# Two attention layers' projections: from whole-array stages to streams of four tiles, with folded spin weights

## Reference

```python
h = emb[x]                                       # token ids -> 2048 rows of 256
q, k, v = h @ Wq.T + bq, h @ Wk.T + bk, h @ Wv.T + bv      # 16 heads of 16
h = (softmax(q k^T / 4) v) @ Wo.T + bo           # attention 1 ("tok")
y = layernorm(h)
q, k, v = y @ Wq.T + bq, y @ Wk.T + bk, y @ Wv.T + bv      # attention 2 ("attn")
s  = q @ Wqs.T + bqs                             # 3 numbers per head
c  = cross(k @ Wks.T + bks, v @ Wvs.T + bvs)
h  = h + softmax((q k^T + s c^T) * temp) v @ Wo.T + bo
```

## Time and profile before

| | us |
|---|---|
| median of 3 runs | 4443.97 (4440.75 to 4445.12) |
| profiled execution | 4443.18, its span 4441.2 |
| busy in the span: PE, DVE, ACT, POOL | 4048.9, 3197.5, 2627.5, 1930.9 |
| first score of attention 1 | 128.03 |
| end of attention 1 | about 536.0 |
| first score of attention 2 | 735.01 |
| end of attention 2 | about 1143.5 |
| rest (output projection 2, feed-forward, recurrence, six layers) | 3298 |

### The profile page before, as it was taken

One profiled execution on the slowest core, in us unless ns is written; L12 is line 12 of the kernel. 1 busy time (PEld: TensorE's weight loads), 2 busy tenths in 40 slices (PEclk: granted clock), 3 DMA queues, 4 the chain that ended last, 5 costly groups with the idle time before them and its releaser, 6 DMA issues. The chain is left out here.

```text
span 4441.2 us, 98171 instructions
## 1 busy us (share of the span) xinstructions
PE 4048.9 (91%) x33142; PEld 2813.6 (63%) x33144; DVE 3197.5 (72%) x5533; ACT 2627.5 (59%) x7011; POOL 1930.9 (43%) x1276
## 2 busy tenths in 40 slices
PE   4899967999445699999999999999999999999997
PEld 2566633666313377777777777777777777777776
DVE  3788644888677677777777777777777777777775
ACT  1476522677231476666666666666666666666664
POOL 2000010000000566666566666665666666666663
PEclk9899987999777899999999999999999999999999
DMA  4222023221010310021011110111001100111001
GB/s 114 73 54 57 21 66 81 55 53 48 20 40 29 104 23 18 20 59 40 18 23 46 46 27 18 39 41 40 20 21 49 51 18 20 51 42 29 20 18 48
DMA packets 101814, 184.23 MB, mean 41 GB/s; under 512 B 25173, under 2 KB 59121, under 8 KB 100977
## 3 DMA queue, kind: packets, MB, share of 16 engines
q1 hardware_dynamic: 100592, 176.37, 14.9%
q0 software_dynamic: 768, 2.10, 0.3%
HBM read 99.51 MB, written 25.17 MB: 28 GB/s over the span
## 5 line engine op out<-in xcount | busy, mean ns | idle before, releaser
L1542 POOL TENSOR_TENSOR swp<-raw,table 128x512 f32<-128x512 f32 x384 | 481.1, 1275 | 635.0 <-DVE ss L1953 634.9
L705 DVE TENSOR_REDUCE maxima<-PS 128x1 f32<-128x512 f32 x1024 | 631.6, 680 | 129.9 <-PE PS L539 129.5
L1625 PE MATMUL PS<-wqk,xT 128*128 128x512 f32 x1536 | 686.5, 600 | 5.7 <-DMA wqk<-in_L_ffn_Wqkv 4.4
L1572 POOL TENSOR_TENSOR probs<-probs,prob_recip 128x512 f32<-128x512 f32 x384 | 472.7, 1250 | 437.5 <-DVE prob_recip L2011 437.5
L1882 ACT ACTIVATE probs<-probs,neg 128x128 f32<-128x128 f32 x1536 | 595.9, 389 | 27.1 <-DVE neg L2005 25.6
L669 ACT ACTIVATE probs<-PS 128x512 f32<-128x512 f32 x1024 | 519.2, 602 | 153.8 <-PE PS L553 153.3
L1552 POOL TENSOR_TENSOR rinv<-ssm,power 128x32 f32<-128x32 f32 x96 | 526.9, 5489 | 0.0
L1625 PEld LDWEIGHTS PS<-wqk,xT 128*128 128x128 f32 x1536 | 283.7, 190 | 336.0 <-issue 253.0
L1728 PE MATMUL PS<-xnT,w 128*128 128x128 f32 x3840 | 476.9, 275 | 0.4 <-DVE hidden L2071 0.4
L539 PE MATMUL PS<-k_stack,q_stack 128*128 128x512 f32 x1024 | 428.1, 438 | 36.4 <-DMA k_stack<-L_attn_qk 17.8
L1728 PEld LDWEIGHTS PS<-xnT,w 128*128 128x128 f32 x3840 | 452.3, 192 | 1.4 <-issue 0.7
(11 more groups left out here) (231 smaller groups left out, 8089.2 us busy)
## 6 DMA issues: line engine op xcount, KB each, us to landing
V_window<-V SPq DMA_DIRECT2D x180, 256.0 KB, 2.8
wqk<-in_L_ffn_Wqkv SPq DMA_DIRECT2D x12, 1024.0 KB, 6.4
w<-in_L_ffn_W SPq DMA_DIRECT2D x18, 640.0 KB, 4.7
q_stack<-L_tok_qk SPq DMA_DIRECT2D x128, 80.0 KB
k_stack<-L_tok_qk SPq DMA_DIRECT2D x128, 80.0 KB
q_stack<-L_attn_qk SPq DMA_DIRECT2D x128, 80.0 KB
k_stack<-L_attn_qk SPq DMA_DIRECT2D x128, 80.0 KB
wv<-in_L_ffn_Wqkv SPq DMA_DIRECT2D x6, 1024.0 KB, 5.1
```

What stands on the lines that cost most here:

```text
L705: dve.tensor_reduce(maxima[:, k // 2, k % 2:k % 2 + 1], SM(r, k), AX.X, ALU.max).then_inc(sm_maxed, 1)
L1542: pool.tensor_tensor(swp[:, w, :, a:a + LD // 2], raw[:, w, :, b:b + LD // 2], table[:, j % 2, 2 + w, a:a + LD // 2].rearrange("p (o d) -> ...
L1572: pool.tensor_tensor(view, view, psr[:, 4 * q:4 * q + 4].rearrange("p (h o) -> p h o", o=1) .to_broadcast([P, 4, P]), ALU.mult).then_inc(p ...
L1625: mm = pe.matmul(wide(kind, half, j), xT[:, k, at:at + P], rhs, start=(k == 0), stop=(k == DC - 1))
```

## The change

`softmax_attention`, `project`, `embed` and `load_constants` go; `attentions` calls `token_projections`, `attend`, `spin_projections`, `attend`, `output_projection`.

- `token_projections` is one block. The ids are loaded first, then constants and all weights of both attentions. Each pair of tiles has its own gather semaphore; PE interleaves transposes (`turn`), query/key units and values by pair. ACT fills the two ring tensors with zeros (two operations), DVE fills V's pads, and after chunk 0 the upper 32 partitions of `ks` with ones. Values are added with their bias two tiles at a time. Behind the 16 units' stores SP issues the loads of heads 0 to 5 in the same block.
- `spin_projections` is one block with attention 1's output projection (pairs of tiles, one PSUM bank), layernorm by chunk (GpSimd's power on 4 columns), and attention 2's projections by chunk. The five spin weights are multiplied into the projection weights once (`fold`), so that the five spin products take XT as input; the feature-major values (L351, L385) go. ACT does the copies of transposes. The spin stores are in two groups of six. It too ends with the loads of heads 0 to 5.
- `attend` leaves the loads of heads 0 to 5 out. Stacks have 16 or 19 rows, no rows of zeros or ones are stored; the row of the maxima is partition 127, and the products for the maxima use partitions 0 to 111 or 0 to 114. `output_projection` serves attention 2 alone, with the bias added ahead of the wait.

```diff
-ROWS = 20
...
+def stack_loads(c, eng, at, scratch, it, r, rows, loaded):
+    qs, ks = at
+    for blk in range(4):
+        for dst, part in ((qs, blk // 2), (ks, 2 + blk % 2)):
+            eng.dma_start(dst[32 * blk:32 * blk + rows, r, :].bitcast(F32),
+                          scratch[part, bass.ds(it, 1), 0:rows, :].rearrange("o r s -> (o r) s")).then_inc(loaded[r], 16)
...
+def token_projections(c, V, qs, ks, scratch, loaded, w, spin_w):
...
+                    load_output_weights(c, sp, "L0_tok", w, wo_loaded)
+                    load_spin_weights(c, sp, spin_w)
+                for n, (ch, which, m) in enumerate(units):
+                    b, off = ch // 2, (ch % 2) * CH
+                    it0 = b * HEADS + m * HPC
+                    for half, (src, ready) in enumerate(((high, qk_high), (low, qk_low))):
+                        sp.wait_ge(ready, n + 1)
+                        sp.dma_start(scratch[2 * which + half, it0:it0 + HPC, 0:HD, off:off + CH],
+                                     src[:, n % 2, :].bitcast(F32)).then_inc(stored[n % 2], 16)
+                for u in range(2):
+                    sp.wait_ge(stored[u], 32 * len(units) // 4)
+                sp.wait_ge(cleared, 3)
+                for r in range(RING):
+                    stack_loads(c, sp, (qs, ks), scratch, r, r, HD, loaded)
+                for u in range(2):
+                    sp.wait_ge(stored[u], 32 * len(units) // 2)
+                sp.wait_ge(wo_loaded, 32)
...
+                turn(0)
+                turn(1)
+                for ch in range(CHUNKS):
+                    for u in range(4):
+                        query_key(4 * ch + u)
+                        if u in (0, 2) and ch + 1 < CHUNKS:
+                            turn(2 * ch + 2 + u // 2)
+                        if u in (1, 3):
...
+                nothing = c.ident[:, :].rearrange("p (o f) -> p o f", o=1).to_broadcast([P, RING * SEQ // P, P])
+                act.activation(qs[:, :, :].rearrange("p r (a f) -> p (r a) f", f=P), nothing, ACT.Copy, scale=0.0).then_inc(cleared, 1)
+                act.activation(ks[:, :, :].rearrange("p r (a f) -> p (r a) f", f=P), nothing, ACT.Copy, scale=0.0).then_inc(cleared, 1)
...
+                    act.wait_ge(qk_done, n + 1)
+                    wait(act, qk_low, n - 1)
+                    wait(act, stored[n % 2], 32 * (n // 2))
+                    act.activation(whole[:, n % 2, :], c.PS[:, 4 + n % 2, :], ACT.Identity, bias=bias, scale=by).then_inc(qk_whole, 1)
+                    act.activation(high[:, n % 2, :], c.PS[:, 4 + n % 2, :], ACT.Identity, bias=bias, scale=by).then_inc(qk_high, 1)
...
+                dve.memset(V[:, :, :, HD:HD + 1], 1.0)
+                dve.memset(V[:, :, :, HD + 1:VW], 0.0)
...
+                for ch in range(CHUNKS):
+                    for u in range(4):
+                        if u in (1, 3) and ch + 1 < CHUNKS:
+                            take(2 * ch + 2 + u // 2)
+                        split(4 * ch + u)
+                        if u in (1, 3):
+                            add_bias(2 * ch + u // 2)
+                    if ch == 0:
+                        dve.wait_ge(cleared, 2)
+                        dve.memset(ks[96:P, :, :].bitcast(F32), 1.0).then_inc(cleared, 1)
...
+def spin_projections(c, V, qs, ks, scratch, loaded, context, w, s):
...
+                    if n % 4 == 3:
+                        for which2 in range(2):
+                            sp.wait_ge(spin_split, 2 * ch + which2 + 1)
+                            for half, src in enumerate((s_high, s_low)):
+                                for comp in range(3):
+                                    sp.dma_start(scratch[2 * which2 + half, b * HEADS:(b + 1) * HEADS, HD + comp, off:off + CH],
+                                                 src[32 * comp:32 * comp + HEADS, which2, :].bitcast(F32)).then_inc(spin_stored, 16)
+                for u in range(2):
+                    sp.wait_ge(stored[u], 32 * len(units) // 4)
+                sp.wait_ge(spin_stored, 16 * 12 * CHUNKS // 2)
+                for r in range(RING):
+                    stack_loads(c, sp, (qs, ks), scratch, r, r, HD + 3, loaded)
...
+                def out_projection(g):
+                    pe.wait_ge(c_taken, g + 1)
+                    wait(pe, added, g)
...
+                def fold(i):
+                    wait(pe, fold_out, 2 * (i - 1))
+                    for d in range(DC):
+                        for k in range(DC):
+                            pe.matmul(c.PS[:, 6 + i % 2, d * 96:(d + 1) * 96], s["raw"][:, origin[i], k, d * P:(d + 1) * P], s["stacks"][:, i, k, :],
+                                      start=(k == 0), stop=(k == DC - 1))
...
+                def spin(ch, i):
+                    n = spins * ch + i
+                    if n < 2:
+                        pe.wait_ge(fold_out, 2 * spins)
+                    wait(pe, spin_out, n - 1)
+                    for k in range(DC):
+                        mm = pe.matmul(c.PS[0:96, 6 + n % 2, :], folded[:, i, k, :], XT[:, ch % 2, k, :], start=(k == 0), stop=(k == DC - 1))
...
+                def project_chunk(ch):
+                    query_key(4 * ch)
+                    spin(ch, 0)
+                    query_key(4 * ch + 1)
+                    spin(ch, 1)
+                    values(2 * ch)
+                    query_key(4 * ch + 2)
+                    spin(ch, 2)
+                    query_key(4 * ch + 3)
+                    spin(ch, 3)
+                    values(2 * ch + 1)
+                    spin(ch, 4)
+                def out_chunk(ch):
+                    turn("c", 2 * ch)
+                    turn("c", 2 * ch + 1)
+                    out_projection(2 * ch)
+                    out_projection(2 * ch + 1)
+                out_chunk(0)
+                out_chunk(1)
+                pe.wait_ge(s["loaded"], 16 * SPIN_LOADS)
+                for i in range(spins):
+                    fold(i)
+                turn("x", 0)
+                turn("x", 1)
+                out_chunk(2)
+                project_chunk(0)
+                turn("x", 2)
+                turn("x", 3)
+                out_chunk(3)
+                project_chunk(1)
+                turn("x", 4)
+                turn("x", 5)
+                project_chunk(2)
+                turn("x", 6)
+                turn("x", 7)
+                project_chunk(3)
...
+                def split_spins(ch, which, src):
+                    wait(dve, spin_stored, 16 * 12 * ch)
+                    dve.tensor_copy(s_high[:, which, :], src).then_inc(spin_high, 1)
+                    dve.wait_ge(spin_high, 2 * ch + which + 1)
+                    dve.tensor_tensor(s_low[:, which, :], src, s_high[:, which, :].bitcast(F32), ALU.subtract).then_inc(spin_split, 1)
...
+                def project_chunk(ch):
+                    split(4 * ch)
+                    dve.wait_ge(spin_out, spins * ch + 1)
+                    split_spins(ch, 0, five[:, 0, :])
+                    split(4 * ch + 1)
+                    add_bias(2 * ch)
+                    split(4 * ch + 2)
+                    split(4 * ch + 3)
+                    add_bias(2 * ch + 1)
+                    cross_products(ch)
+                    split_spins(ch, 1, cross[:, :])
...
+                out_chunk(0)
+                dve.wait_ge(s["loaded"], 16 * SPIN_LOADS)
+                dve.tensor_scalar(bqs[:, :], s["bqk"][:, 0, :], s["factor"][:, 0:1], None, ALU.mult).then_inc(scaled, 1)
+                norm(0)
+                out_chunk(1)
+                for i in range(spins):
+                    dve.wait_ge(fold_done, i + 1)
+                    dve.tensor_copy(folded[:, i, :, :], c.PS[:, 6 + i % 2, 0:DC * 96].rearrange("p (d n) -> p d n", d=DC)).then_inc(fold_out, 1)
+                    dve.tensor_tensor(fold_bias[:, i:i + 1], c.PS[0:96, 6 + i % 2, DC * 96:DC * 96 + 1], s["sbias"][:, i:i + 1], ALU.add).then_inc(fold_out, 1)
+                dve.wait_ge(fold_out, 2 * spins)
+                dve.tensor_scalar(fold_bias[:, 0:1], fold_bias[:, 0:1], s["factor"][0:96, 0:1], None, ALU.mult).then_inc(scaled, 1)
+                out_chunk(2)
+                norm(1)
+                project_chunk(0)
+                norm(2)
+                out_chunk(3)
+                project_chunk(1)
+                norm(3)
+                project_chunk(2)
+                project_chunk(3)
...
+    KMAX = 96 + rows
...
-                sp.dma_start(qs[0:1, r, :].rearrange("o (a t) -> o a t", a=QT).bitcast(F32),
+                sp.dma_start(qs[P - 1:P, r, :].rearrange("o (a t) -> o a t", a=QT).bitcast(F32),
...
-                if h0:
+                if h0 and not (isinstance(t, int) and t < RING):
...
-                pe.matmul(SM(r, k), qs[:, r, q * P:(q + 1) * P], ks[:, r, half * CH:(half + 1) * CH],
+                pe.matmul(SM(r, k), qs[0:KMAX, r, q * P:(q + 1) * P], ks[0:KMAX, r, half * CH:(half + 1) * CH],
...
+            attentions(c)
```

(28 more changed lines are left out.)

594 lines of the change are left out of this document (373 added, 221 removed).

## The result

The changed kernel takes 4773.22 us (median of four runs, 4771.72 to 4778.74) where the kernel before takes 4442.36 (four runs, 4438.96 to 4445.12): a ratio of 1.0747 [1.0729, 1.0766], 331 us slower. 4363 had been forecast, with a range of 4342 to 4392. The prediction was wrong, in sign and far outside its range.

The account below looks back on a forecast made before the run. PE bounds the attention loops, which stay; PE's idle time in the projection stretches was to shrink. 4443.2 - 27.5 (part A) - 53.6 (part B) = 4362.1 us, 4363 as median, range 4342 to 4392.

Parts of the forecast that it names:

- What costs nothing: Attention loops and second output projection: fewer stack rows and the loads cost nothing, loops stay at 408 us.
- Part B: End of attention 1 to first score of attention 2: 145.4 us instead of 199.0, a gain of 53.6.
- 48 loads, 17.9: Stack loads of six heads ending the block before attention 2: 17.9 us, at a pitch of 0.373 us.
- wrong if: Signs of failure: chunk period above 26, fold over 12 us, clock in B under 0.9, a score waiting for a load.
- part A: Start to first score of attention 1: 100.5 us instead of 128.0, a gain of 27.5.
- rival (b): Less gain: first gathers stand behind 3 MB of weights, B's chunks still paced by stores; 4389 us, chance 0.15.
- rival (a): More gain: store cycle shortens to PE's 2.9 us, loads issue at 0.33, allowances unused; about 4345 us, chance 0.15.
- The fills: Part A: ACT's two ring fills 5.5 us each, off the path; DVE's fill of `ks` 5.2, 3.4 on the path.
- Rival (c): Slower: short pauses keep PE at 1.2 GHz throughout the projections; 4502 us, chance 0.05.
- the row of the pitch: Stack loads: 0.373 us per 80 KB load is the issuing queue's time, so 48 issues hold the block 17.9 us.

Follow-up runs that it names:

- E1: The changed kernel with attention 2's loads at 20 rows instead of 19, the added row zeros stored once at the start: 4363.32 us.
- D1: E1 with 17 rows in attention 1 and 21 in attention 2 instead of 16 and 20: 4705.24 us.
- D2: E1 with 18 rows in attention 1 and 24 in attention 2 instead of 16 and 20: 4384.62 us.
- E4: The changed kernel with each 19-row load of attention 2 issued as two, of 16 and 3 rows: 4376.88 us.
- E5: E1 with only head 0 loaded ahead of each attention, heads 1 to 5 at the head of the loop: 4333.34 us.
- E6: E5 with head 0's eight loads put among the last stores of each projection block: 4324.03 us, 0.9733 of the kernel before.
- E3: The kernel before with loads of 19 rows instead of 20 in attention 1 alone: 4834.85 us.
- E2: The changed kernel with attention 2's scratch laid out in planes of 20 rows, loads still taking 19: 4772.78 us.

## Why the prediction was wrong, step by step

**The step that failed** is "What costs nothing": "Rows of the stacks fall from 20 to 16 or 19 ... the loads of the loop are hidden (DMA share 0.20, rows 1)". I asked what fewer rows cost PE and took it for granted that a load with less data can't take longer. The share of 0.20 was read as slack of a whole; how many of the 16 engines one load uses was never asked. The same fault is in Part B's "48 loads, 17.9": the 0.373 us of the earlier trace rows belongs to loads of 20 rows, and the new ones are not of that kind. With 19 rows, 129 us took the place of 17.9, and 710 that of 408. No rival held this; the "wrong if" did name the symptom (a score that waits for a load in spite of the prefetch). The trace of before had a hint, in the row of 729.5 us above: loads alone, issued faster than they land, and still a share of 0.64 (80 KB every 0.373 us are 220 GB/s issued, and 147 were moved). The price of the cause, 76 KB at one engine's pace, stands in no row of before.

**The rest of the sum held, in part by luck.** E1 has the 20 rows for which the sum was in effect made, and takes 4363.32 us; the sum gave 4363. By the marks of the table above, E1 gains 29.0 us in part A (27.5 forecast) and 55.8 in part B (53.6), and loses 2.7 in the two loops and 2.9 in the rest, where the sum had nothing; the differences nearly cancel. The parts, in the trace of after:

- Part A: first score at 100.70, forecast 100.5, but errors cancel. The first ACT copy came at 23.40 (21.6 forecast). From it to the sixteenth took 51.3 us, not 57.7, and the last store was out at 77.16 instead of 82.0. The 48 loads gave the 5 us back: with 16 rows their pitch is 0.48 us, not the 0.373 of 20 rows, 22.9 us instead of 17.9.

```profile
23.40 0.69 ACT L258 ACTIVATE whole<-PS,bqs 128x512 f32<-128x512 f32 x1 [8.56 <-issue]
...
34.91 0.69 ACT L258 ACTIVATE whole<-PS,bqk 128x512 f32<-128x512 f32 x1 [7.99 <-DMA tok_qk<-low]
...
42.12 5.18 DVE L311 MEMSET k_stack<- 32x6144 f32 x1 [1.34 <-issue]
...
50.24 0.69 ACT L258 ACTIVATE whole<-PS,bqk 128x512 f32<-128x512 f32 x1 [5.72 <-DMA tok_qk<-low]
...
74.74 0.69 ACT L258 ACTIVATE whole<-PS,bqk 128x512 f32<-128x512 f32 x1 [0.45 <-PE PS L219]
...
76.83 0.33 SPq L180 DMA_DIRECT2D tok_qk<-low  x1
77.28 0.38 SPq L132 DMA_DIRECT2D q_stack<-tok_qk  x1
```

- The 51.3 us are themselves a sum in which errors cancel. The step to the third unit takes 9.25 us instead of 3.48, since ACT waits for the first unit's store: 5.8 us lost, where 2 were allowed for sharing with the weights. The DMA share is 0.93 from 22 to 36 us, and with more stores of zeros ahead this wait grows (none in after, 8.0 us; 12 in D1, 12.5 us; 28 in D2, 24.6 us), so rival (b)'s queue was there, though at the first stores and not at the gathers. The step to the seventh unit takes 6.99, since the `low` of the fifth unit, whose store it waits for, is made only behind DVE's fill: 3.5 lost, 3.4 forecast. The 13 other steps take 2.70 us each and not 3.48, PE's pace: 10.1 gained. That is rival (a)'s mechanism, against which I had set that nothing in these DMAs changes. Something did: the planes went from 20 rows to 16, and SP issues a store in 0.33 us instead of 0.60 (see D2).
- The fills: 5.18 us on DVE against 5.2 taken from GpSimd's row, and ACT's two 5.3 each against 5.5. The Trainium skill (VectorE: DVE Perf Modes, section Zero memsets can be issued as uint32) gave an estimate of 6.4 us for this fill; the trace has 5.18, which decides.
- Part B: five folds took 6.6 us, 1.3 each, not 1.6. The first query product is 31.4 us behind the end of attention 1 (30 forecast), chunks start 26.3, 20.8 and 20.9 us apart, and PE is done after 118.8 us (120.5). No copy of ACT waits for a store here; the stores did not pace the chunks, and so that half of rival (b) falls:

```profile
528.00 1.36 PE L470 MATMUL PS<-spin_w,spin_raw 128*128 128x96 f32 x8
...
534.60 1.07 PE L434 MATMUL PS<-ident,X 128*128 128x128 f32 x8
...
541.93 1.88 PE L451 MATMUL PS<-XT,spin_wq 128*128 128x512 f32 x4
```

- Rival (c), the clock, did not occur where it was looked for: 0.97 in the projections of B. It shows up in attention 2 (0.80), behind a wait that had another cause.
- The Trainium skill's rule against the row of the pitch (DMA: Bandwidth & Descriptors, section Issuing engines are not separate DMA queues): E4, E5 and E6 show that issues do decide when these blocks end. With 40 fewer of them ahead of each attention, the first score of attention 1 comes 16.4 us sooner. The rule, that an issue is usually small beside its transfer, is true of the 19-row loads (0.23 us beside 2.97) and not of what a block of 48 costs.

## What to carry to other kernels

Before changing how many rows a DMA moves, find the largest divisor up to 16 of the number of rows: 20 rows, one of them zeros, came at 141 GB/s where 19 came at 26. A DMA share near a sixteenth while loads queue is the sign of it, and so is an issue of microseconds on a queue whose issues took tenths. And a prefetch at the end of a block costs its issues on the path: load what the first consumer needs, put it among the last stores, and leave the rest to the loop.

## What the runs showed of the hardware that was not expected

- A load from memory on one DMA engine ran at 26 GB/s, and ten engines reached 141 to 147 GB/s, or 14 each; sixteen were no faster than ten (124 GB/s), and 24 rows, on twelve engines, gave the most, 167. Whether the issues or the memory set the upper figures was not separated.
- SP's time to issue one load rose with the engines, from 226 ns for one to 365 for sixteen (table above). 20 rows were issued faster than 16.
- The slow loads held SP in the issue itself, and what stood behind waited too. The small DMA that places a head's row of maxima (`neg_row`) took at most 0.74 us to issue in the kernel before; in the changed kernel it took up to 3.54 us and in E3 up to 5.56.
- SP's time to issue a q/k store of 256 KB was 0.33 us into planes of 16 rows and 0.59 to 0.61 into planes of 17, 18, 19, 20 and 24 (D1, D2, after, the kernel before).
- GpSimd's second gather took 3.42 us while DVE filled V, and the third 0.95. Fill and gather ended close together, at 9.17 and 10.07 us. The traces of E1, E2, E4, E5, E6, D1 and D2 have the same pair (3.41 or 3.42 us); in the kernel before, without a fill, the second gather took 0.95. No run moved the fill away:

```profile
5.91 3.26 DVE L294 MEMSET V<- 128x3840 f32 x1 [0.73 <-issue]
6.65 3.42 POOL L195 DMA_INDIRECT X<-in_L_tok_emb,row  x1 [0.30 <-issue]
...
10.37 0.95 POOL L195 DMA_INDIRECT X<-in_L_tok_emb,row  x1 [0.30 <-issue]
```
